# Splitting the FFN weights in place and turning them by DMA, with the next pair's norm moved to earlier stages

## The reference, cut to what matters

```python
# 16 batches; x: (16, 256, 1024), ctx: (16, 256, 512)
x = x + tanh(g_xattn) * attention(layernorm(x), ctx, masks)
x = x + tanh(g_ffn) * ffn(layernorm(x))

def attention(x, y):            # channels 256, 8 heads of 32 channels
    q, k = conv(y, wq, bq) * mask_cond, conv(y, wk, bk) * mask_cond   # weights standardised by row
    v = conv(x, wv, bv) * mask
    scores = softmax(q k^T / SCALE)              # 32 x 32 per head, over channels
    out = conv(scores v, wo, bo) * mask + x
    return (norm of out over channels * gamma + beta) * mask

def ffn(x):                     # 4096 tokens of 1024
    top 2 of 8 routes: gates from softmax(x wr^T)
    h = silu(silu(x w1^T) w3^T) w2^T             # w1, w3, w2: 1024 x 1024, the same for all routes
    out[route] += gate * h                       # rows 0 to 7 of the output
```

## Time and profile before

| | |
|---|---|
| median of 3 runs | 1165.01 us (1164.57 to 1166.37) |
| the profiled execution | 1164.77 us |
| its span, first instruction to last | 1163.0 us |
| TensorE, VectorE, ScalarE, GpSimd busy | 91%, 69%, 40%, 36% of the span |
| mean granted clock of TensorE | 0.97 of full |
| one steady pass | 127.5 us (514.87 to 642.34) |

### The profile page before, as it was taken

One profiled execution on the slowest core, in us unless ns is written; L12 is line 12 of the kernel. 1 busy time (PEld: TensorE's weight loads), 2 busy tenths in 40 slices (PEclk: granted clock), 3 DMA queues, 4 the chain that ended last, 5 costly groups with the idle time before them and its releaser, 6 DMA issues.

```text
span 1163.0 us, 17830 instructions
## 1 busy us (share of the span) xinstructions
PE 1056.6 (91%) x6627; PEld 608.0 (52%) x6627; DVE 806.0 (69%) x1913; ACT 466.8 (40%) x714; POOL 415.6 (36%) x500
## 2 busy tenths in 40 slices
PE   4566279899999999999999999999999999999998
PEld 2355145564556555564556555655556455654452
DVE  6787457896679747986689657975788658973221
ACT  4456333345242633354243533353234524262331
POOL 2472002481147403671158212750167114730000
PEclk9778589999999999999999999999999999999999
DMA  8801700017100540027001620035001700054000
GB/s 269 219 19 55 216 1 1 1 63 188 42 1 27 135 128 0 18 78 192 0 0 36 172 80 0 18 117 153 0 0 72 213 4 0 0 142 149 1 1 2
DMA packets 102753, 81.82 MB, mean 70 GB/s; under 512 B 69342, under 2 KB 87332, under 8 KB 102716
## 3 DMA queue, kind: packets, MB, share of 16 engines
q1 hardware_dynamic: 100656, 79.77, 23.5%
q10 hardware_dynamic: 2060, 1.58, 0.5%
HBM read 47.75 MB, written 16.81 MB: 56 GB/s over the span
## 4 chain that ended last, share of the span: by engine, by line
PE 55%; DVE 23%; POOL 8%; issue 8%; ACT 5%; DMA 1%; ACTq 1%; POOLq 0%; DVEq 0%
PE bank L655 38%; PE bank L531 7%; DVE ub L1206 6%; DVE ub L1225 3%; DVE ub L1221 2%; PE bank L542 2%; POOL xbuf L394 2%; POOL mtmp L391 2%; POOL coc L355 2%; DVE bst L1161 2%; PE bank L554 1%; DVE bst L1216 1%; ACT h_hi L900 1%; DVE act_t L1318 1%; DVE x_hi L1172 1%
## 5 line engine op out<-in xcount | busy, mean ns | idle before, releaser
L655 PE MATMUL bank<-xt_hi,w1b 128*128 128x512 f16 x1024 | 326.7, 381 | 0.0
L655 PE MATMUL bank<-w3b,h_hi 128*128 128x512 f16 x1024 | 304.5, 379 | 0.5 <-DVE act_t L1318 0.5
L655 PE MATMUL bank<-xt_lo,w1b 128*128 128x512 f16 x512 | 194.9, 381 | 0.0
L655 PE MATMUL bank<-w3b,h_lo 128*128 128x512 f16 x512 | 194.0, 379 | 0.0
L894 ACT ACTIVATE act_t<-bank,fs 128x512 f32<-128x512 f32 x128 | 87.1, 680 | 193.8 <-PE bank L655 193.7
L1323 DVE SCALAR_TENSOR_TENSOR h_lo<-act_t,h_hi 128x512 f16<-128x512 f32 x128 | 98.4, 769 | 91.7 <-ACT h_hi L900 91.7
L900 ACT ACTIVATE h_hi<-act_t 128x512 f16<-128x512 f32 x128 | 80.8, 632 | 199.2 <-DVE act_t L1318 199.2
L655 PEld LDWEIGHTS bank<-xt_hi,w1b 128*128 128x128 f16 x1024 | 100.6, 98 | 114.3 <-issue 2.1
L1318 DVE SCALAR_TENSOR_TENSOR act_t<-act_t,bank 128x512 f32<-128x512 f32 x128 | 86.2, 673 | 102.0 <-ACT act_t L894 101.8
L655 PEld LDWEIGHTS bank<-w3b,h_hi 128*128 128x128 f16 x1024 | 98.0, 98 | 76.6 <-DVE act_t L1318 0.5
L410 POOL TENSOR_TENSOR ub<-bo_b,mcur 128x512 f32<-128x512 f32 x64 | 64.6, 1039 | 163.8 <-DVE dg L1183 163.8
(11 more groups left out here) (200 smaller groups left out, 1814.6 us busy)
## 6 DMA issues: line engine op xcount, KB each, us to landing
xbuf<-in_x_dram SPq DMA_DIRECT2D x16, 1024.0 KB, 8.6
out_dram<-xbuf SPq DMA_DIRECT2D x16, 1024.0 KB, 4.2
x_lo<-in_ctx_dram SPq DMA_DIRECT2D x16, 512.0 KB, 3.5
mrow<-in_mask_dram SPq DMA_DIRECT2D x16, 512.0 KB, 4.3
w1b<-in_w_dram SPq DMA_DIRECT2D x8, 512.0 KB, 7.3
w3b<-in_w_dram SPq DMA_DIRECT2D x8, 512.0 KB, 7.7
xbuf<-in_w_dram SPq DMA_DIRECT2D x1, 4096.0 KB, 13.6
xt_hi<-x_hi SPq DMA_TRANSPOSE x32, 4.1
```

What stands on the lines that cost most here:

```text
L655: mm = pe.matmul(bk[:, :], left, right, start=d == 0 and n == 0, stop=d == FT - 1 and n == 2)
```

## The change

Weights. w1 is loaded by rows like they lie in memory, w3 as before. ScalarE scales and rounds a whole block of 128x1024 to fp16 (`w_high`) into one of five slots, which lie in h1 and h2, not needed yet; VectorE writes the low half (`w_low`); SP turns both halves by two DMA transposes into the place of the block's fp32 rows (`turn`). Blocks 0 to 4 are split in the prologue, 5 to 15 in groups 0 to 6 of pass 0. TensorE waits for a block's turn in front of its group, and in front of group 8 for all of w3. TensorE's transposes of weights and their banks go.

Prologue. Batch 1 projects into other banks (att 0 and 1, fbk 1, rbk), some orders change, the norm's steps come earlier or later, ctx's largest for pair 1 is spread by TensorE instead of GpSimd's reduction, tokens are issued by SP ahead of the stores, and the router of pass 0 follows group 1 as in the others.

Stages. VectorE's `ln1` goes to stages 1 and 2, GpSimd's to 2 and 3, ScalarE's `normed` to 2 and 3, `x_high` to 3 and 4, `x_low` to 3 and 4, and `add_beta` to 5 and 6, where each batch's waits for its `ub_ready`; `values` stays alone in 7 and 8. `tokens_high` makes both the rounded and the plain tokens from x, a half at a time.

```diff
+    def w_slot(i):
+        return ((3, 0), (4, 0), (0, 0), (1, 0), (2, 0), (0, 1), (1, 1), (2, 1),
+                (0, 2), (1, 2), (2, 2), (0, 3), (1, 3), (2, 3), (0, 4), (0, 5))[i]
+
+    def w_blocks(g):
+        return {0: (5, 6, 7), 1: (8, 9), 2: (10, 11), 3: (12, 13), 4: (14,), 6: (15,)}.get(g, ())
...
# SyncE
+            def turn(i):
+                slot, used = w_slot(i)
+                sp.wait_ge(sm["w_lo"], i + 1)
+                for part, w in zip(w_part, (w1_hi, w1_lo) if i < FT else (w3_hi, w3_lo)):
+                    sp.dma_start(w[:, i % FT, :].rearrange("c (f p) -> c f p", f=FT), part[slot], transpose=True)\
+                        .then_inc(w_turned[slot], 16)
             def pair(j, last=False):
                 load_x(j)
+                if j == 1:
+                    for i in range(FT, 2 * FT):
+                        turn(i)
...
+            for b in range(2):
+                tokens(0, b)
+                turn(b)
             store(0)
-            tokens(0)
+            for i in range(2, FT):
+                turn(i)
...
# GpSimd
-                if s in (3, 4):
-                    ln1(2 * j + s - 3)
-                if s in (2, 3):
-                    bias_part(2 * j + s - 2, s - 2)
+                if s == 2:
+                    pool.wait_ge(sm["s_ready"], 2 * j + 1)
+                    bias_part(2 * j, 0)
+                    ln1(2 * j)
+                if s == 3:
+                    ln1(2 * j + 1)
+                    x_low(2 * j, 0)
+                    bias_part(2 * j + 1, 1)
+                if s == 4:
+                    x_low(2 * j + 1, 1)
                 if s in (5, 6):
-                    x_low(2 * j + s - 5, s - 5)
-                if s == 7:
-                    add_beta(j, 0, 0)
-                    values(2 * j, 0)
-                    add_beta(j, 0, 1)
-                    add_beta(j, 1, 0)
-                if s == 8:
-                    values(2 * j + 1, 1)
-                    add_beta(j, 1, 1)
+                    pool.wait_ge(sm["ub_ready"], 2 * j + s - 4)
+                    add_beta(j, s - 5, 0)
+                    add_beta(j, s - 5, 1)
+                if s in (7, 8):
+                    values(2 * j + s - 7, s - 7)
...
-            y_largest(1)
...
# TensorE
+                    if d == 0 and first_pair(j):
+                        slot, used = w_slot(g)
+                        pe.wait_ge(w_turned[slot], 32 * (used + 1))
...
-            for t in range(TT):
-                long_product(1, 1, t)
-            for i in range(4, 8):
-                weight(i)
-            for n in range(4):
-                attention_back(0, 0, n)
-            for i in range(8, 12):
-                weight(i)
...
# ScalarE
+            def w_high(i):
+                slot, used = w_slot(i)
+                if i % FT == 0:
+                    act.wait_ge(sm["w_scale"], 2 + i // FT)
+                need(act, w_turned[slot], 32 * used)
+                src = w1n[:, i, :] if i < FT else w3n[:, i - FT].rearrange("p f c -> p (f c)")
+                act.activation(w_part[0][slot], src, ACT.Copy, scale=sc[:, i // FT, 2:3]).then_inc(sm["w_hi"], 1)
...
-                if s in (4, 5):
-                    normed(2 * j + s - 4, s - 4, co, sm["ln1_coef"], sm["xs_ready"])
+                if s in (2, 3):
+                    normed(2 * j + s - 2, s - 2, co, sm["ln1_coef"], sm["xs_ready"])
...
# VectorE
+            def w_low(i):
+                slot, used = w_slot(i)
+                dve.wait_ge(sm["w_hi"], i + 1)
+                src = w1n[:, i, :] if i < FT else w3n[:, i - FT].rearrange("p f c -> p (f c)")
+                dve.scalar_tensor_tensor(out=w_part[1][slot], in0=src, scalar=sc[:, i // FT, 2:3], in1=w_part[0][slot],
+                                         op0=ALU.mult, op1=ALU.subtract).then_inc(sm["w_lo"], 1)
...
                     for t in range(CT):
+                        if s == 2 and t == 2:
+                            ln1(j, 1)
                         qk_out(2 * j + s // 2, s // 2, t)
                 if s in (1, 3):
                     softmax(2 * j + s // 2, s // 2)
+                if s == 1:
+                    ln1(j, 0)
                 if s in (3, 4):
                     t1_low(2 * j + s - 3)
-                    ln1(j, s - 3)
+                    x_high(2 * j + s - 3, s - 3)
                 if s in (5, 6):
                     bias_tiles(2 * j + s - 5, s - 5)
-                    x_high(2 * j + s - 5, s - 5)
...
                 if ja is not None and g > 0:
                     attention(ja, g - 1)
                 if w3:
-                    for i in w3_banks(g, middle=True):
-                        weight(i)
-                if g == (ROUTER_FIRST if w3 else ROUTER)[2]:
-                    gates(j)
+                    for i in w_blocks(g):
+                        w_low(i)
                 ffn(j, g)
```

More of the change, by code:

```diff
@@ L435, in _ @@
                 coefs(n, mvc[:, 4 * n:4 * n + 4], coc[:, :, 4 * n:4 * n + 4], 4, EPS, 1.0, "ws", None)
+            bias_part(0, 0)
             ln1(0)
[L437 removed]
+            x_low(0, 0)
             ln1(1)
[L439 removed]
+            add_beta(0, 0, 0)
+            x_low(1, 1)
             bias_part(1, 1)
[L441 to L442 removed]
             add_beta(0, 0, 1)
@@ L499, in smalls_transposed, with project @@
                 for d in range(FT):
-                    last = pe.transpose(fbk[1][:, NE * d:NE * d + NE], wrf[:, P * d:P * d + P], ident[0:NE, 0:NE])
+                    last = pe.transpose(fbk[0][:, 3 * P + NE * d:3 * P + NE * d + NE], wrf[:, P * d:P * d + P], ident[0:NE, 0:NE])
                 last.then_inc(sm["wr_tr"], 1)
[L503 to L520, removed]
+            def project(q, b, t, bk=att):
                 if t == 0:
@@ L649, in ffn @@
                         pe.wait_ge(sm["h_lo"], GROUPS * j + d + 1)
+                    if g == FT and d == 0 and first_pair(j):
+                        for slot, n in enumerate((6, 4, 4)):
+                            pe.wait_ge(w_turned[slot], 32 * n)
                     k, f = (g - FT) // 2, slice(TOK * (g % 2), TOK * (g % 2) + TOK)
@@ L865, in tokens_high @@
             def tokens_high(q, b):
-                normed(q, b, co2, sm["ln2_coef"], sm["xs2_ready"])
-                act.wait_ge(sm["xs2_ready"], q + 1)
-                act.activation(tok_hi[b], xs[b], ACT.Copy).then_inc(sm["tok_hi_set"], 1)
+                act.wait_ge(sm["ln2_coef"], q + 1)
+                for c in range(CH):
+                    for x, done in ((tok_hi, "tok_hi_set"), (xs, "xs2_ready")):
+                        act.activation(x[b][:, c, :], xa[b][:, c, :], ACT.Identity, bias=co2[:, 3, c:c + 1],
+                                       scale=co2[:, 2, c:c + 1]).then_inc(sm[done], 1)
             def attention(j, s):
@@ L913, in group @@
                 if w3:
-                    for i in w3_banks(g, middle=True):
-                        weight(i)
-                if w3 and g == FT:
-                    act.wait_ge(sm["fs_set"], 2)
+                    for i in w_blocks(g):
+                        w_high(i)
+                    if g in (0, 2, 4, 6, FT):
+                        n = (0, 2, 4, 6, FT).index(g)
+                        act.wait_ge(w_turned[(3, 4, 1, 2, 0)[n]], (32, 32, 128, 128, 192)[n])
+                    if g == FT:
+                        act.wait_ge(sm["fs_set"], 2)
                 ffn(j, g)
@@ L1208, in bias_tiles, with attention_out @@
                 ins.then_inc(sm["ub_ready"], 1)
-            def attention_out(q, b):
-                dve.wait_ge(sm["ub_ready"], q + 1)
+            def attention_out(q, b, ts=range(TT)):
+                if ts[0] == 0:
+                    dve.wait_ge(sm["ub_ready"], q + 1)
                 def stats(t):
@@ L1216, in stats @@
                     dve.bn_stats(bst2[:, t, :], u[b][:, t, :]).then_inc(sm["u_stat"], 1)
-                for t in range(TT):
+                for t in ts:
                     bk = att[t % 4]
@@ L1436, in _ @@
+            y_low(0, 1)
+            small_largest()
+            below_largest(0, 0)
+            biases()
+            v_low()
+            block_weights(0, 0)
+            w_row(0)
+            dve.wait_ge(sm["ws_copy"], 3)
+            for t in range(CT):
+                qk_out(1, 1, t, bk=(att[0], att[1], fbk[1], rbk))
+            ln1(0, 0)
+            t1_low(0)
+            small_scale()
             small_low()
-            t1_low(0)
             ln1(0, 1)
+            below_largest(1, 1, bk=fbk[1])
@@ L1448, in _ @@
             weight_scale(0)
-            for i in range(4):
-                weight(i)
-            attention_out(1, 1)
-            for i in range(4, 8):
-                weight(i)
+            attention_out(1, 1, range(1, TT))
             residual(0, 0)
-            for i in range(8, 12):
-                weight(i)
+            w_low(0)
+            residual(1, 1)
             tokens_low(0, 0)
-            residual(1, 1)
+            w_low(1)
             tokens_low(1, 1)
```

(2 more changed lines are left out.)

342 lines of the change are left out of this document (169 added, 173 removed).

## The result

The changed kernel takes 1182.31 us (median of 4 runs, 1181.19 to 1182.73) against 1164.87 for the kernel before beside it: 1.46% slower, ratio 1.0146 with an interval of 1.0128 to 1.0163. The forecast was 1161, range 1136 to 1180. The profiled execution took 1181.19, its span 1179.3, 16.3 us more than before.

The account below looks back on a forecast made before the run. TensorE, busy 91% of the span, was taken as the bound, so time leaves only where it waits or runs at low clock. 1164.8 - 22 (prologue and pass 0) + 18 (six steady passes) gave 1161 us, range 1136 to 1180.

Parts of the forecast that it names:

- The first two parts: Prologue: group 1 earlier by 31.5 us; pass 0 gives part back, leaving -22 for both.
- part 3: Six steady passes: waits removed, normed and add_beta waits added; +3 us a pass, +18 in all.
- The hold by `add_beta`: Steady pass, stages 5 and 6: GpSimd's add_beta delays VectorE's bias_tiles and tile 4, +2.7 to +5.4 us before offsets.
- The low clock behind the wait: Steady pass: clock falls behind a TensorE gap of some 5 us, 1.5 us; counted only in a rival.
- the tokens ahead of the stores: Prologue: SP issues a batch's tokens before the stores, saving 1.5 us, between 0 and 3.
- The sum of VectorE's chain: Pass 0: VectorE's work from its first eviction at 133.5 to tile 4 of stage 7, 75 us.
- Removed waits: Steady pass: the wait for x_lo (0.8) and most of that at L608 (1.1) go, 1.9 us.
- New ones from `normed`: Steady pass, stages 2 and 3: ScalarE's normed delays scores, t1, exp and cb, 1.5 us uncovered.
- With one L1206 per instruction: Steady pass: one VectorE operation per GpSimd instruction; batch 1's eight end about 12.0 us behind batch 0's ub_ready.
- rival B: Steady passes: add_beta holds VectorE once per instruction throughout and the clock falls, +5.9 a pass, 1178 us; chance 0.22.
- Rival A: Steady passes: add_beta slips between VectorE's operations, tile 4 no longer waits, 1.6 us won a pass, 1133 us; chance 0.24.
- Rival C: Pass 0 starves on turned blocks: -10 in place of -22, with +18, 1173 us; chance 0.12.

Follow-up runs that it names:

- the experiment with old stages: Changed kernel's weights, prologue and pass 0 router, but norm, halves and add_beta in the stages of the kernel before: 1136.45 us, ratio 0.9755.
- the one with stores first: Kernel with add_beta a batch later, plus SP issuing both stores of pair 0 before the tokens in the prologue: 1125.72 us against 1125.12.
- The first experiment: Changed kernel with batch 0's add_beta waiting for batch 1's ub_ready and batch 1's split around values: 1125.12 us, ratio to before 0.9659.
- the experiment with `normed`: Kernel with add_beta a batch later, plus ScalarE's normed of batch 1 moved to stage 4, behind cb: 1123.03 us.
- the second experiment: Changed kernel with add_beta's instructions replaced by GpSimd memsets, product with beta left out from pair 1 on: 1123.93 us, one run.
- the last experiment: Kernel with add_beta a batch later and normed behind cb, plus w3's block 15 split in group 5, not 6: 1120.51 us, ratio 0.9613.

## Why the prediction was wrong

The first two parts held, the sum did not. It failed in part 3, at two terms of a steady pass. The hold by `add_beta` was taken at the middle of its range, +3 a pass with the other waits, and came at its upper end, +4.6. The low clock behind the wait was put at nothing in the sum, and cost 1.5 a pass. Together the pass shown above lost 6.1, and the mean of six 5.95, in place of 3: that is 17.7 of the 20 us between the forecast and the profiled execution; the other 2.6 are pass 0 and the end.

- Prologue: group 0 at 115.5 was forecast, 115.53 came. That it agrees to 0.03 is luck: other executions with the same prologue have it from 114.20 on, and the tokens ahead of the stores, counted at 1.5, made 2.2 to 3.5. Pass 0's tile 4 at 208.8, came at 209.84; -21 was -20.0. The sum of VectorE's chain held: 134.06 to 209.84 are 75.8 us (75 counted), 63.4 of them busy. Its reading did not go far enough: the experiment with old stages shows that 7.2 of pass 0's lengthening belong to the stages, and the one with stores first that a start of group 0 some 3 us later costs 1.6 by pass 1 and 0.6 in the medians.
- Removed waits: `x_lo` (0.8) and L608 (1.1) went as forecast. New ones from `normed`: 1.5 counted, 0.9 + 0.2 came.
- `add_beta`: the prediction gave 615.7 to 618.4 for a tile that was at 613.02, "With one L1206 per instruction" or "with two", and took the middle, +3 a pass. The trace shows one per instruction: six of the eight L1229 are held, 1.25 to 1.48 us each, until `add_beta` ends. The other terms stood. Batch 0's `ub_ready` comes 9.1 us before TensorE wants tile 4 (593.50, 602.58), as the forecast 602.6 does for 611.78, so neither `bias_part` nor what was moved ahead made it later than counted. From there to the end of the eight are 11.8 us, 12.0 forecast, and the L1354 behind them takes 1.0 more (0.9 forecast). The wait is 6.63 = 1.24 + 5.4, the upper end to the tenth. Two in a gap are nowhere in the earlier trace rows; the semaphore gap of 0.08 us was given a weight that no row supported.
- The clock: 1.5 us a pass stood only in rival B. It follows from the wait: 0.51 for 3 us behind it, and filling the wait gives 1.6 back. The two together are the +5.9 that B had (six passes, 35; measured 35.7), so B was the case that came, given 0.22, and with pass 0 at -20 and not -22 it ends just above the range.
- Rival A did not come. The first experiment shows what it would have been worth: a pass of 125.1, 2.4 below the kernel before where A had 1.6. The forecast for A also left out what pass 0 would gain, so it is 1125 and not 1133.
- Rival C had a small part: TensorE stood 2.99 us in front of group 8 (4.18 in the experiment with `normed`, where splitting the last block a group earlier took the wait away), but not in three groups.

The Trainium skill, page "SBUF — State Buffer", section "Who interferes with whom", says that a VectorE instruction with two SBUF inputs contends with a GpSimd instruction that reads SBUF and not with one that only writes it. The trace agrees: 8.62 us beside the tensor operations, 3.25 beside the memsets of the second experiment. Read strictly, as the prediction wrote, it stood for the upper end, and the wait came out there; the 1169 that the prediction gave by it is 12 below the profiled 1181.19, 9 of them the clock.

## What to carry to other kernels

Where GpSimd gets elementwise work that reads SBUF, look at which VectorE instructions with two SBUF operands stand beside it, and count one of them held per GpSimd instruction; beside `add_beta` the VectorE operations that read one of two operands from PSUM were not held here (L1245 0.41, L1349 0.68). Moving `add_beta` later by a batch turned 1.5% slower into 3.4% faster. When a range has an end that every row of the trace supports and another that only a hope does, take the former, and put the clock's price into the sum where a TensorE wait grows by microseconds (1.5 to 1.6 us a pass behind waits of 3.1 and 6.6 here).

## What was not expected of the hardware

A TensorE wait of 3.1 us was followed by the lower clock (0.50 for 2.6 us, 1.6 us lost a pass) just as one of 6.6 was; behind waits of 1.24 and 1.48 us the clock stayed at 1.00. Pass 0 has some between: behind the 2.00 us at tile 4 in the last experiment it stayed at 1.00, behind 2.32 us in front of group 8 in the first experiment it was 0.68, in mean, over the next 2.6 us (windows view of the two):

```profile
201.88:204.48 2.60, 2.60 (x20) 2.08 (x21) 2.60 (x8) 0.00 (x0) 2.44 (x3) 1.00 0.00 0
```

```profile
198.44:201.00 2.56, 2.56 (x13) 1.57 (x14) 1.86 (x5) 0.63 (x1) 1.63 (x2) 0.68 0.02 6
```

GpSimd's memsets of 0.95 us held up nothing on VectorE.
